# Addresses of expert tiles read in bulk into registers, and a row slot for every tile of the second list

## The reference

```python
logits = x @ gate_w.T                       # 14 experts
probs = jax.nn.softmax(logits, axis=-1)
top2_p, top2_i = jax.lax.top_k(probs, 2)
w = top2_p / jnp.maximum(top2_p.sum(-1, keepdims=True), 1e-10)
hh = jax.nn.gelu(jnp.einsum('nd,edf->nef', x, w1) + b1, approximate=False)
all_out = jnp.einsum('nef,efd->ned', hh, w2) + b2
moe_out = w[:, 0:1] * all_out[n, top2_i[:, 0]] + w[:, 1:2] * all_out[n, top2_i[:, 1]]
x = layernorm(x + clip(x + moe_out, -100, 100))
```

## Time and profile before

| | |
|---|---|
| Median of the runs | 433.38 us (431.49 to 434.42) |
| Span of the profiled execution | 485.0 us |
| TensorE busy | 364.4 us, 75% |
| VectorE busy | 323.4 us, 67% |
| GpSimd busy | 289.2 us, 60% |
| ScalarE busy | 263.2 us, 54% |
| GpSimd, scatters to `results` (line 757) | 77, 76.8 us |
| VectorE, copies of weights (line 1100) | 77 |

### The profile page before, as it was taken

One profiled execution on the slowest core, in us unless ns is written; L12 is line 12 of the kernel. 1 busy time (PEld: TensorE's weight loads), 2 busy tenths in 40 slices (PEclk: granted clock), 3 DMA queues, 4 the chain that ended last, 5 costly groups with the idle time before them and its releaser, 6 DMA issues. The chain is left out here.

```text
span 485.0 us, 12845 instructions
## 1 busy us (share of the span) xinstructions
PE 364.4 (75%) x4145; PEld 268.7 (55%) x4145; DVE 323.4 (67%) x1056; ACT 263.2 (54%) x624; POOL 289.2 (60%) x455
## 2 busy tenths in 40 slices
PE   4666998877897788889877686663968868778770
PEld 3434565555565455556544446563857757676570
DVE  7766587777886778677867746442636766662396
ACT  2026676676677667666755575432446445434054
POOL 7403365687768776876755447856555655566271
PEclk9679999899989999899988989877788897988995
DMA  5322334334333433342301312222422222220663
GB/s 138 99 71 70 89 93 124 94 92 131 98 98 96 129 97 95 101 124 79 107 24 57 59 46 57 77 55 73 131 73 81 61 67 73 71 80 3 201 212 108
DMA packets 72974, 44.02 MB, mean 91 GB/s; under 512 B 13233, under 2 KB 68931, under 8 KB 72796
## 3 DMA queue, kind: packets, MB, share of 16 engines
q1 hardware_dynamic: 66650, 33.11, 25.8%
q0 software_dynamic: 4640, 9.36, 6.0%
q10 hardware_dynamic: 1618, 0.73, 0.6%
HBM read 18.54 MB, written 12.36 MB: 64 GB/s over the span
## 5 line engine op out<-in xcount | busy, mean ns | idle before, releaser
L890 ACT ACTIVATE probs<-S 128x768 f32<-128x768 f32 x128 | 103.8, 811 | 59.9 <-PE S L1518 34.9
L757 POOL DMA_INDIRECT results<-tile_rows x77 | 76.8, 998 | 57.8 <-DVE tile_rows L1109 38.8
L1238 DVE TENSOR_REDUCE row_max<-S 128x4 f32<-128x1024 f32 x64 | 78.0, 1218 | 23.3 <-PE S L1553 20.2
L803 POOL DMA_INDIRECT sorted_rows<-x,row_no x64 | 65.6, 1025 | 35.9 <-DVE row_no L1270 22.0
L1572 PE MATMUL O<-probs,flat 128*32 128x256 f32 (+1 forms) x1024 | 58.8, 350 | 0.3 <-DVE row_chosen L1284 0.3
L1510 PE MATMUL S<-q_stack,k_stack 64*128 64x256 bf16 (+1 forms) x512 | 44.8, 254 | 16.6 <-ACT probs L890 14.0
L776 POOL TENSOR_SCALAR_AFFINE_SELECT probs<-probs 128x256 f32<-128x256 f32 x104 | 39.9, 407 | 23.5 <-ACT probs L890 23.2
L1238 DVE TENSOR_REDUCE row_max<-M 128x8 f32<-128x1024 f32 (+1 forms) x32 | 39.0, 1219 | 10.9 <-PE M L1553 10.9
L1572 PEld LDWEIGHTS O<-probs,flat 128*32 128x32 f32 x1024 | 27.8, 113 | 23.2 <-issue 7.4
L880 ACT ACTIVATE hT<-S,k_stack 128x128 f32<-128x128 f32 x76 | 24.8, 370 | 27.3 <-PE S L1618 14.0
L1547 PE MATMUL S<-k_stack,q_stack 64*128 64x256 bf16 (+1 forms) x320 | 27.4, 268 | 16.2 <-DVE row_max L1238 13.6
(11 more groups left out here) (271 smaller groups left out, 895.4 us busy)
## 6 DMA issues: line engine op xcount, KB each, us to landing
q_stack<-flat SPq DMA_DIRECT2D x96, 64.0 KB
k_stack<-flat SPq DMA_DIRECT2D x85, 64.0 KB
tile_rows<-sorted_rows SPq DMA_DIRECT2D x77, 64.5 KB
experts<-in_L_ffn_w_dram SPq DMA_DIRECT2D x28, 128.0 KB
xin<-in_L_attn_target_dram SPq DMA_DIRECT2D x16, 128.0 KB, 2.8
xres<-in_L_attn_target_dram SPq DMA_DIRECT2D x16, 128.0 KB
out_dram<-probs SPq DMA_DIRECT2D x8, 256.0 KB, 2.3
q_stack<-results SPq DMA_DIRECT2D x7, 256.0 KB, 3.2
```

Of the source, the lines that this page charges most:

```text
L757: pool.indirect_dma_start(results, bass.IndirectOffsetOnAxis(ap=y_rows[:, slot, D:ROW].bitcast(U32), axis=0), y_rows[:, slot, 0:D], None, ...
L803: pool.indirect_dma_start(sorted_rows, bass.IndirectOffsetOnAxis(ap=row_no[:, q * 2 * TT + n:q * 2 * TT + n + 1], axis=0), x2[:, q, n % 2, ...
L890: act.activation(probs[:, n].rearrange("p (a q) -> p a q", a=2), S[0][:, :].rearrange("p (a q) -> p a q", a=2)[:, :, 0:T + P], ACT.Exp, sc ...
L1238: dve.tensor_reduce(row_max[:, s % R, :, g0:g0 + ng, half], maxima_of[i][:, :].rearrange("p (a h k) -> p a h k", a=2, h=ng), X, ALU.max).t ...
```

## The change

**Tables.** `pack` becomes `make_bytes`: two operations instead of six. One writes for each tile the byte at which its block of rows begins (`rows_byte`), the other the column at which its expert's weights begin (`weights_no`). Nothing is packed. The constants for packing go.

**Reads.** `bytes_of` reads a table into registers, 24 tiles with one load, so that each tile's address stands in a register of its own. VectorE reads 30 registers right behind the first table and 47 at the end of list 1, ahead of list 2; SyncE reads the same numbers at its own places. The reads carry no bounds check.

**Row slots.** In list 2 each of the 47 tiles has a slot of its own in `late`. SyncE issues the loads in groups of 1, 1, 2, 2, 3, 3, then 4 each and 3; each group has one of six semaphores, and TensorE waits for the whole group. From the seventh group on SyncE waits until TensorE has transposed the tiles of the group six before. SyncE also waits for the last product that reads `probs`.

**Row numbers.** In list 2 VectorE no longer copies them; GpSimd's indirect DMA takes them from the row slot. The wait for a free result slot moves in front of the bias addition. List 1 keeps its six slots and its copies.

```diff
-    LISTED = -(-K2 // XR) * XR
+    GROUPS = (1, 1, 2, 2, 3, 3) + (4,) * 8 + (3,)
...
+        late_rows = late[:, 0:K2 * ROW].rearrange("p (n c) -> p n c", c=ROW)
+        def rows_of(s):
+            return rows[:, s % XR] if s < K1 else late_rows[:, s - K1]
...
-        def experts_of(eng, turn):
-            return eng.value_load(expert_word[0:1, bass.ds(turn, 1)], min_val=0, max_val=(1 << EXPERT_BITS * XR) - 1)
-        def expert(word, q):
-            return ((word >> EXPERT_BITS * q) & ((1 << EXPERT_BITS) - 1)).with_bounds(min_val=0, max_val=E - 1)
+        def group_of(n):
+            g = 0
+            while sum(GROUPS[:g + 1]) <= n:
+                g += 1
+            return g, sum(GROUPS[:g + 1])
+        def group_count(g):
+            return 16 * (K1 // XR) + 16 * sum(GROUPS[g % XR:g + 1:XR])
+        def bytes_of(engine, table, first, n, limit):
+            out = []
+            for at in range(first, first + n, 24):
+                out.extend(nc.values_load_multi_w_load_instructions(
+                    table[0:1, at:min(at + 24, first + n)], engines=[engine], min_val=0, max_val=limit,
+                    skip_runtime_bounds_check_because="the table is made with a min against the highest block and expert")[1])
+            return out
...
# SyncE
-            def load_rows(s, q, turn, is_tile):
-                if is_tile(s):
-                    if q % 2 == 0:
-                        blocks[0] = first_blocks[s // 2] if s // 2 in first_blocks else blocks_of(s // 2)
-                    n = (blocks[0] >> BLOCK_BITS * (q % 2)) & ((1 << BLOCK_BITS) - 1)
-                    n = n.with_bounds(min_val=0, max_val=E * (REGION // P))
-                    wait_apart(sp, rows_turned, s - XR + 1, ids_copied)
-                    sp.dma_start(rows[:, q], sorted_rows[bass.ds(n * P, P)]).then_inc(rows_in[q], 16)
+            def load_rows(s, at):
+                n = row_bytes[bass.ds(at, BLOCK_BYTES)].rearrange("(p c) -> p c", p=P)
+                return sp.dma_start(rows_of(s).bitcast(U8), n)
+            first_rows = bytes_of(mybir.EngineType.SP, rows_byte, 0, K1, blocks)
...
             for s in range(K1):
-                early_tile(load_rows)(s)
+                after(sp, rows_turned, s - XR + 1)
+                after(sp, ids_copied, s - XR + 1)
+                load_rows(s, first_rows[s]).then_inc(rows_in[s % XR], 16)
...
             sp.wait_ge(words_done, 4)
+            later_rows = bytes_of(mybir.EngineType.SP, rows_byte, K1, K2, blocks)
...
-            run_tiles(sp, load_rows)
+            sp.wait_ge(pv_done, 4 * B)
+            for g, tiles_in in enumerate(GROUPS):
+                if g >= XR:
+                    sp.wait_ge(rows_turned, K1 + sum(GROUPS[:g - XR + 1]))
+                for n in range(sum(GROUPS[:g]), sum(GROUPS[:g]) + tiles_in):
+                    load_rows(K1 + n, later_rows[n]).then_inc(rows_in[g % XR], 16)
...
# GpSimd
-                    pool.indirect_dma_start(results, bass.IndirectOffsetOnAxis(ap=y_rows[:, slot, D:ROW].bitcast(U32), axis=0),
+                    ids = y_rows[:, slot, D:ROW] if s - 5 < K1 else rows_of(s - 5)[:, D:ROW]
+                    pool.indirect_dma_start(results, bass.IndirectOffsetOnAxis(ap=ids.bitcast(U32), axis=0),
...
# VectorE
-                    if q == 0:
-                        word[0] = experts_of(dve, turn)
-                    e = expert(word[0], q)
                     after(dve, y_biased, s - XR + 1)
-                    dve.tensor_copy(expert_now[q], experts[:, bass.ds(e * SIZE, SIZE)]).then_inc(expert_ready, 1)
-                if is_tile(s - 1):
+                    dve.tensor_copy(expert_now[q], experts[:, bass.ds(weights_at[s], SIZE)]).then_inc(expert_ready, 1)
+                if is_tile(s - 1) and s - 1 < K1:
...
                 if is_tile(s - 5):
+                    if s - 5 >= K1:
+                        dve.wait_ge(sent[(s - 5) % YR], 16 * ((s - 5) // YR))
...
-            def pack(of, n, word0, block0, lists):
+            def make_bytes(of, first, n, lists):
                 dve.wait_ge(tile_turned, lists)
...
+                dve.tensor_scalar(rows_byte[:, first:first + n], of[0:1, P:P + n], float(E * (REGION // P)), float(BLOCK_BYTES),
+                                  ALU.min, ALU.mult).then_inc(words_done, 1)
+                dve.tensor_scalar(weights_no[:, first:first + n], of[0:1, 0:n], float(E - 1), float(SIZE),
+                                  ALU.min, ALU.mult).then_inc(words_done, 1)
+            def load_weights_at(first, n, lists):
+                dve.wait_ge(words_done, 2 * lists)
+                weights_at.extend(bytes_of(mybir.EngineType.DVE, weights_no, first, n, (E - 1) * SIZE))
...
                 if t == B + 2:
-                    pack(M[1], K1, 0, 0, 1)
+                    make_bytes(M[1], 0, K1, 1)
+                    load_weights_at(0, K1, 1)
...
             early_tile(layers)(AFTER)
-            pack(G, LISTED, WORDS1, BLOCKS1, 2)
+            make_bytes(G, K1, K2, 2)
             for s in range(AFTER + 1, K1 + 5):
                 early_tile(layers)(s)
-            dve.wait_ge(words_done, 4)
+            load_weights_at(K1, K2, 2)
             run_tiles(dve, layers)
...
# TensorE
-                    pe.wait_ge(rows_in[q], 16 * (turn + 1))
+                    if s < K1:
+                        pe.wait_ge(rows_in[q], 16 * (turn + 1))
+                    else:
+                        g, _ = group_of(s - K1)
+                        pe.wait_ge(rows_in[g % XR], group_count(g))
                     after(pe, rows_copied, s if s < K1 else s - 1)
-                    pe.transpose(turned(s), rows[:, q, 0:D], ident[:, :]).then_inc(rows_turned, 1)
+                    pe.transpose(turned(s), rows_of(s)[:, 0:D], ident[:, :]).then_inc(rows_turned, 1)
```

More of the change, by code:

```diff
@@ L54, in transformer_layer @@
     K2 = TILES - K1
-    LISTED = -(-K2 // XR) * XR
-    assert K1 % XR == 0 and K1 <= LISTED <= P and (2 * G1 * T - E * (P - 1)) > (K1 - 1) * P
-    WORDS1, WORDS = K1 // XR, (K1 + LISTED) // XR
-    BLOCKS1, BLOCKS = K1 // 2, (K1 + LISTED) // 2
+    assert K1 % XR == 0 and K1 <= P and K2 <= P and (2 * G1 * T - E * (P - 1)) > (K1 - 1) * P
+    GROUPS = (1, 1, 2, 2, 3, 3) + (4,) * 8 + (3,)
+    assert sum(GROUPS) == K2
     PIECES = 8
@@ L68, in transformer_layer @@
     YR = 10
-    EXPERT_BITS = 4
-    BLOCK_BITS = 10
-    assert E <= 1 << EXPERT_BITS and EXPERT_BITS * XR <= 24
     assert 17 * (E - 1) < 1 << 8 and REGION // P == 33
-    assert REGION % P == 0 and E * (REGION // P) < 1 << BLOCK_BITS and XR % 2 == 0
+    assert REGION % P == 0
+    BLOCK_BYTES = P * ROW * 4
     def on(s):
@@ L631, in _ @@
             sp.wait_ge(words_done, 2)
[L633 to L651 removed]
+            row_bytes = sorted_rows.rearrange("n c -> (n c)").bitcast(U8)
+            blocks = E * (REGION // P) * BLOCK_BYTES
+            def load_rows(s, at):
+                n = row_bytes[bass.ds(at, BLOCK_BYTES)].rearrange("(p c) -> p c", p=P)
+                return sp.dma_start(rows_of(s).bitcast(U8), n)
+            first_rows = bytes_of(mybir.EngineType.SP, rows_byte, 0, K1, blocks)
             for i in range(R):
@@ L660, in _ @@
             sp.wait_ge(words_done, 4)
-            for w in range(BLOCKS1, BLOCKS1 + XR // 2):
-                first_blocks[w] = blocks_of(w)
+            later_rows = bytes_of(mybir.EngineType.SP, rows_byte, K1, K2, blocks)
             for i in range(R):
@@ L1046, in numbers @@
                                       float(REGION // P - 1 + 2 * a), None, ALU.mult).then_inc(numbered, 1)
-                for q in range(XR):
-                    dve.memset(expert_unit[:, q:q + 1], float(1 << EXPERT_BITS * q)).then_inc(numbered, 1)
-                for q in range(2):
-                    dve.memset(block_unit[:, q:q + 1], float(1 << BLOCK_BITS * q)).then_inc(numbered, 1)
             def masks_below():
```

45 lines of the change are left out of this document (8 added, 37 removed).

## The result

The changed kernel takes 453.6 us in the median (449.85 to 456.71), beside 433.56 for the kernel before in the same comparison (431.49 to 434.42): a ratio of 1.0426, 95% interval 1.0377 to 1.0475 (taken without the slowest and profiled run, 456.71 us, which is why it is not 453.6 / 433.56). That is slower by 4%, where I had 438.6 us and a range that ended at 446.

The account below looks back on a forecast made before the run. GpSimd's scatter pace, 1.28 us per tile, was taken to bound list 2. Seam +5.0, attention +2.0, single reads -1.3 and second packing -0.5 summed to +5.2: 438.6 us on 433.38, range 423 to 446.

Parts of the forecast that it names:

- 0.19 + 0.13n: Bulk reads on VectorE: forecast cost in us of reading n registers, 6.5 for 47 in two reads, 4.3 for 30.
- seam +5.0: Between list 1 and list 2: the 47-register read delays VectorE's first weight copy, so TensorE waits 5.0 us longer.
- Rival 3: Registers dearer than forecast: 449.6 us at the full single-read price, 443.6 halfway (0.215 us per register); chance 0.14.
- nothing in the trace shows trips that overlap: Reason given for pricing a bulk read of n registers as n separate trips to memory, 0.13 us each on VectorE.
- Rival 1: Bulk reads cost 0.6 us whatever the count, so the seam is not delayed: about 431.5 us; chance 0.33.
- The 30-register read: In attention, behind the first packing: 4.3 us on VectorE, heads' reciprocals up to 2.95 us late, +2.0 carried.
- GpSimd's 1.28 us covers it: 0: List 2: GpSimd's scatter pace hides VectorE's row-number copies, so dropping them gains 0; uncovered, up to 9 us.
- Rival 2: VectorE bounds list 2 in timed runs, saving 9.0 us: 422.5 with cheap reads, 429.6 with the forecast's; chance 0.15.
- The pauses of 2 us every 7 us: GpSimd's stops between list 2 bursts, taken as belonging to the profiled execution; timed runs should need about 60 us.
- SyncE's second bulk read: 47 registers near the end of list 1: 6.4 us, over before the loaded rows are needed, so 0.
- single reads gone -1.3: List 1: five single register reads leave VectorE, 0.5 us each, half of it beside engine work: -1.3 us.
- second packing -0.5: List 2's table: six small VectorE operations become two, about 0.5 us less.

## Why the prediction was wrong

**The price of a register** was the step on which the seam hung. I split the single read and took 0.19 + 0.13n; the reads took 0.237 and 0.224 us per register at the seam (5.69 for 24, 5.16 for 23), and the term "seam +5.0" measured +10.2. Rival 3's halfway case (0.215, +8.6) was nearest. The Trainium skill's 200 ns per register ("Runtime: NRT & Kernel Launch", section on instruction fetch mechanics) agrees with the 210 that SyncE took alone. What my split does not have, nor the rule, is that the price depends on where the table part begins: at a multiple of 16 bytes it is 66 ns on SyncE and 78 on VectorE (1.86 us for 24). My 0.13 holds in neither case. The sentence "nothing in the trace shows trips that overlap" was true and told nothing: the trace had no read of two words. Rival 1 (cheap whatever the count) fell as well, since even the best 24 registers take 1.59 us.

**The 30-register read** has the opposite failure: 2.85 us against 4.3 forecast, but 7.2 us lost in the traces against the +2.0 carried. In the medians it is less: undoing it gave 3.8 us (read moved) and 4.6 (matmuls in the gap), and a loss of about 4 is what is left of the 20 between the medians when the other marks are taken off; that the trace shows more fits an execution 3 us above its median. I followed the delay to the heads' reciprocals rightly and then added it as a delay. What it did was let TensorE stand idle for 3.42 us, and behind this the granted clock was at the lower level (0.50 from 263 to 278). The run with the 26 unread matmuls shows that this is most of the cost: by the marks of the two traces 5.2 of 7.2 us come back while the read stays where it was. I had not asked what an idle TensorE costs beyond the idle time.

**"GpSimd's 1.28 us covers it: 0"** for the row numbers and single reads in list 2 was the third failed step. I read the 0.71 us copy and the 1.28 us scatter as master and follower. They hold each other up: with 16-column copies the scatters take 0.97 (the longest 1.03). Before the change it is mostly the copy that gives way, after it the scatter, and then the 1.28 is no longer GpSimd's pace. It costs 4.8 us in the changed kernel; and 5.9 us of the median can be had back with two register operations per tile. So the words' arithmetic, which I booked as a cost hidden in the sequencer, was worth something. Row numbers and their earlier wait together come to less (list 2 64.5 with them, 68.3 without), and which of the two does it is open. Rival 2, VectorE as the bound, is wrong: VectorE did get faster (0.99 per tile instead of 1.28, until the result slots were full) and list 2 slower.

The Trainium skill has a page that bears on it ("SBUF — State Buffer", section "SBUF: two separate sides"): VectorE's float32 copies in on-chip memory take a port pair that GpSimd shares, under an exclusive lock for the whole instruction, and GpSimd cannot write the descriptors of its DMA meanwhile. The runs agree that each is stretched by the other (0.97 to 1.68, 0.48 to 0.71), and that the scatter is whole without the copy. A scatter of 1.68 us lies beside two copies of 0.48 and ends 0.13 us behind the second (356.57, 356.44). That the lock passes to GpSimd only when VectorE's queue of such instructions has a gap, and that the arithmetic makes this gap, is my reading and not shown: in the trace the copy starts at the same distance in both cases, and the 0.22 and 0.06 us of the sequencer's rows fit the reading without proving it. So the arithmetic is shown as the cause, by adding it alone, and how it works stays open.

**What held.** The pauses of 2 us every 7 us belong to that execution: in the second trace of before, list 2 takes 61.02 us (forecast: about 60) at mostly 1.28 us per scatter. SyncE's second bulk read was far dearer than forecast (12.5 us against 6.4) and covered as forecast; with it in place and VectorE's undone the time is 434.66. Row loads in groups and the scatter by row-slot numbers are worth 0, as said. The terms "single reads gone -1.3" and "second packing -0.5" cannot be seen: list 1 takes 60.30 against 60.05, and between the traces of all kernels it varies from 57.7 to 62.2.

In the sum: forecast +5.0 +2.0 -1.8 + 0 = +5.2; the marks of the two traces give +10.2 +7.2 +0.3 +0.9 +4.8 -0.1 = +23 between two spans, of which the medians show 20. The range failed because I let rivals vary the price of the read alone, and gave neither of the other two steps a bad end.

No kernel that computes the whole result beats the kernel before by more than its interval (the one with 16-column copies, 0.9935, leaves weights out): with reads made cheap and arithmetic put back the ratio is 0.9997. The ready-made addresses bring nothing that can be measured. That neither engine's sequencer was on the path would explain it; no run shows it by itself.

## What to carry to other kernels

Before a bulk read of registers is placed, see to it that its first word lies at a multiple of 16 bytes and that its count is a multiple of four (7 registers took longer than 8, and 23 longer than 24), and put it where the engine is idle with nothing behind it that feeds TensorE. Price a delay in front of TensorE by the clock it gets afterwards as well as by the wait. Two engines whose instructions are stretched to the same period are not master and follower until one of them has been taken away in a run: making one of them faster can slow the pair.

## What the runs showed of the hardware

- A read of 24 words into registers on SyncE: 1590 ns (66 each) if the first word is at a multiple of 16 bytes, 5040 (210 each) if not; 8 words 693 and 1838. On VectorE 24 took 1.86 us aligned and 5.69 not.
- A count that is no multiple of four is dearer than the next higher one that is, from aligned starts: 2 words 670 ns and 4 words 486 on SyncE; 7 words 1150 and 8 words 593 to 651 on VectorE, 23 words 2215 and 24 words 1829.
- Reads at work beside reads alone, on SyncE in the changed kernel: 24 words from word 30 took 5.44 us, alone 5.04; 24 from word 0 took 1.77, alone 1.59. The 23 words from word 54 took 7.04 us; no run reads these alone, so what made them dearest is open.
- With an idle time of 3.42 us in it, TensorE's granted clock was 0.70 in the stretch 253 to 273 instead of 1.00, a mean of its two levels, and 0.50 from 263 to 278; matmuls of one shape took 537 ns on average in the 20 us instead of 391. With 26 matmuls of no use in the gap it was 1.00.
- GpSimd's scatter and VectorE's copies of 642 columns, which touch different tiles: 0.97 and 0.49 us when the other is away, 0.97 and 0.71 in one rhythm, 1.68 and 0.48 in the other. In this kernel register arithmetic in front of the copy (two operations added alone were enough) decided it: the four traces with it have a list 2 of 61.0 to 61.8 us, those without 64.5 to 68.3.
